# A two-layer gated cross-attention network on one core: maxima taken bank by bank and shared PSUM banks handed round differently in the second attention

## What is computed

```python
x = x + tanh(g_xattn[0]) * _L0_xattn_ref(_layernorm(x), ctx, ...)  # two attentions of 16 heads of 128, rounded to fp8
x = x + tanh(g_ffn[0])   * _L0_ffn_ref(_layernorm(x), ...)         # silu(gate) * up, 704 wide
x = x + tanh(g_xattn[1]) * _L1_xattn_ref(_layernorm(x), ctx, ctx, mask, ...)
x = x + tanh(g_ffn[1])   * _L1_ffn_ref(_layernorm(x), ...)         # 8 experts, the best one for each token

# _L1_xattn_ref: 32 heads of 8 features in 8 groups; keys and values come from ctx
q = (Q @ w_q.T).reshape(B, S, 8, 4, 8); k = (K @ w_k.T).reshape(B, S, 8, 8); v = (V @ w_v.T).reshape(B, S, 8, 8)
scores = einsum('bnghd,bmgd->bnghm', q, k) / sqrt(8)    # then the padding mask and the causal mask
out = einsum('bnghm,bmgd->bnghd', softmax(scores), v).reshape(B, S, 256)
return out @ w_o.T + b_o
```

## Time and profile before

| | us |
|---|---|
| median of 3 runs | 1426.37 (1425.85 to 1427.44) |
| the profiled execution, its own time | 1425.13 |
| its span | 1423.40 |
| PE busy in the span | 1302.0 (91%) |
| DVE, ACT, POOL busy | 1091.0, 952.1, 749.1 |
| mean granted clock of PE | 0.968 of full |

### The profile page before, as it was taken

The page is one execution under the profiler, slowest core; times in us unless marked ns, Lnnn a source line. Parts: engine busy times, 40 slices in busy tenths (PEclk is TensorE's granted clock), DMA queues, the critical chain, the costliest instruction groups (busy, mean ns, idle before and its releaser), DMA issues.

```text
span 1423.4 us, 29539 instructions
## 1 busy us (share of the span) xinstructions
PE 1302.0 (91%) x11516; PEld 1111.9 (78%) x11516; DVE 1091.0 (77%) x2141; ACT 952.1 (67%) x2110; POOL 749.1 (53%) x698
## 2 busy tenths in 40 slices
PE   1587999999999999999999999889998788996998
PEld 1577999999999999999999999767775333444998
DVE  7999888889889889889888888965345555656464
ACT  5897777877877877877887777653222454564675
POOL 5668557556557556656656643330001444453675
PEclk9699999999999999999999999999999898997899
DMA  3201010000000000000100100033544341106562
GB/s 112 60 9 30 17 23 17 16 24 16 17 23 16 24 16 16 29 11 17 31 9 16 57 2 2 16 123 51 73 73 63 69 54 46 46 2 220 181 237 96
DMA packets 59978, 69.76 MB, mean 49 GB/s; under 512 B 6811, under 2 KB 52091, under 8 KB 59712
## 3 DMA queue, kind: packets, MB, share of 16 engines
q1 hardware_dynamic: 56720, 58.64, 16.9%
q0 software_dynamic: 2944, 9.19, 1.8%
q10 hardware_dynamic: 176, 0.04, 0.0%
HBM read 55.56 MB, written 12.34 MB: 48 GB/s over the span
## 4 chain that ended last, share of the span: by engine, by line
PE 66%; DVE 16%; POOL 6%; DMA 4%; issue 4%; ACT 2%; SPq 1%; POOLq 0%; ACTq 0%; DVEq 0%
PE PC L453 7%; PE SS L419 6%; PE PO L435 5%; PE PA L387 4%; PE B L399 4%; PE PA L364 3%; PE B L1079 3%; PE PA L366 3%; PE PO L1063 2%; POOL WR L816 2%; DVE QN L700 2%; PE SS L2056 2%; PE B L2056 2%; PE B L2073 2%; PE PC L2073 2%
## 5 line engine op out<-in xcount | busy, mean ns | idle before, releaser
L873 POOL TENSOR_TENSOR RB<-YS,M 128x512 bf16<-128x512 f32 x128 | 163.5, 1277 | 254.4 <-DVE YS L726 254.4
L548 ACT ACTIVATE QT<-B,sm 128x256 f32<-128x256 f32 x256 | 131.1, 565 | 166.8 <-PE B L399 166.8
L419 PE MATMUL SS<-QT,KT 128*128 128x256 f32 x512 | 154.7, 397 | 9.4 <-DVE mx L681 9.0
L364 PE MATMUL PA<-WH,XQ 128*128 128x256 f32 x512 | 141.1, 307 | 20.9 <-POOL XQ L804 14.9
L869 POOL TENSOR_TENSOR yy<-vv,half 128x12 f32<-128x12 f32 x64 | 146.9, 2296 | 5.3
L366 PE MATMUL PA<-WL,XQ 128*128 128x256 f32 x512 | 130.3, 287 | 0.0
L1687 ACT ACTIVATE P<-PO,mcf 128x1024 f32<-128x1024 f32 x64 | 71.3, 1114 | 86.3 <-PE PO L1548 86.2
L700 DVE TENSOR_TENSOR QN<-QN,yy 128x512 f32<-128x512 f32 x128 | 122.5, 957 | 2.0 <-POOL yy L869 2.0
L1868 POOL TENSOR_SCALAR_AFFINE_SELECT P<-P 128x1024 f32<-128x1024 f32 x64 | 70.1, 1096 | 100.2 <-ACT P L1687 100.2
L681 DVE TENSOR_REDUCE mx<-SS 128x4 bf16<-128x512 f32 x128 | 88.1, 688 | 44.3 <-PE SS L411 44.2
L693 DVE TENSOR_REDUCE vv<-SQ 128x6 f32<-128x768 f32 x128 | 120.6, 943 | 0.0
(11 more groups left out here) (335 smaller groups left out, 4083.3 us busy)
## 6 DMA issues: line engine op xcount, KB each, us to landing
W<-in_w SPq DMA_DIRECT2D x16, 1024.0 KB
Q<-qsc SPq DMA_DIRECT2D x48, 128.0 KB
WR<-in_wprojT SPq DMA_DIRECT2D x16, 256.0 KB, 3.0
K<-ksc SPq DMA_DIRECT2D x12, 256.0 KB
qsc<-T POOLq DMA_DIRECT2D x8, 384.0 KB, 3.0
X<-in_x SPq DMA_DIRECT2D x4, 512.0 KB, 7.8
CR<-in_xctxT SPq DMA_DIRECT2D x8, 256.0 KB, 3.0
RSM<-rsm_d SPq DMA_DIRECT2D x16, 128.0 KB, 4.3
```

What stands on the lines that cost most here:

```text
L364: pe.matmul(PA[:, 256 * k:256 * k + 256], XQ[:, k, c, bs], wh[:, c, 256 * k:256 * k + 256], start=c == 0, stop=False)
L419: pe.matmul(SS[:, 256 * z:256 * z + 256], k[:, 128 * z:128 * z + 128], q[:, 256 * z:256 * z + 256], start=True, stop=False)
L548: a.activation(QT[i % 2][:, o:o + 256], B1[:, o:o + 256], ACT.Identity, bias=col(n + "b"), scale=col(n + "w"))
L873: p.tensor_tensor(RB[i % 2][:], YS[:], M[:], ALU.subtract).then_inc(s_rb, 1)
```

## The change

Nothing is computed otherwise; the order, the banks and the waits change.

1. `pe_shifted` in attention 0: both fp32 pairs first, then the four products with the maxima. As one bank is started only once, the second pair no longer has `start=True`.
2. `dve_maximum_1`: two reductions, one for each bank of PA, each with its own count. From step 8 on `pe_raw` waits for each half right before that half's mask product.
3. `pe_weigh_1` runs ten steps after the raw scores, not eleven, into columns 0 to 255 of B1 (even step) or B2 (odd step); `act_evac_out` copies after every step, half as much.
4. Turned maxima of blocks 2 and later go to columns 256 to 383 of B1, not to SS. The users of SS and PC move to other phases. PE's new order is, for `n % 4` = 0: raw, shifted, weigh, `pe_max_turn`, `pe_out_turn`, `pe_next_turn`; 1: raw, shifted, weigh, `pe_turn_1`, `pe_logits`; 2: raw, shifted, weigh, `pe_out_proj`; 3: raw, shifted, weigh, `pe_turn_1`. ACT copies turned maxima at the start of phase 1.
5. The queries of quarter 2 are projected behind raw step 7 into B1 and B2 (before, ahead of it into PO), those of quarter 3 turned at `n` = 9 through SS and PC (before, at 8 through B1 and B2).
6. SP loads WO and WG at `n` = 12, ahead of the queries of blocks 8 and up.
7. The routing constants are made in feed-forward 0, each in columns of its own of the scratch tile.
8. The statistics of the next layer norm are taken after each residual; the root step only gathers them, and the scaling does one block a step. SP's stores of these rows go out five steps later.

```diff
@@ pe_shifted
             for z in range(2):
                 pe.matmul(SS[:, 256 * z:256 * z + 256], k[:, 128 * z:128 * z + 128], q[:, 256 * z:256 * z + 256],
-                          start=True, stop=False)
-                for h in (2 * z, 2 * z + 1):
-                    t = pe.matmul(SS[:, 128 * h:128 * h + 128], m[:, h:h + 1].broadcast_to([128, 128]), negib[:],
-                                  start=False, stop=h % 2 == 1)
+                          start=z == 0, stop=False)
+            for h in range(4):
+                t = pe.matmul(SS[:, 128 * h:128 * h + 128], m[:, h:h + 1].broadcast_to([128, 128]), negib[:],
+                              start=False, stop=h == 3)
...
@@ turn_banks, proj_banks, dve_feed_forward_0
-            return (SS[:], PC[:]) if q4 == 2 else (B1[:], B2[:]) if q4 == 3 else PAh
+            return (SS[:], PC[:]) if q4 >= 2 else PAh
...
-            return (POa, POb) if q4 == 2 else (SS[:], PC[:]) if q4 == 3 else PAh
+            return (B1[:], B2[:]) if q4 == 2 else (SS[:], PC[:]) if q4 == 3 else PAh
...
+                    if q4 == 1 and n == 2:
+                        dve_routing_constants(v)
...
@@ sp_attention_1
-                if n == 14:
-                    sp.wait_ge(s_down, 16)
-                    sp.wait_ge(s_qst[3], 32)
+                if n == 12:
+                    sp.wait_ge(s_qp, 8)
                     sp.dma_start(WO[:], w1o.rearrange("(c p) n -> p c n", p=128)).then_inc(s_wog, 16)
                     sp.dma_start(WG[:], wgate.rearrange("(c p) n -> p c n", p=128)).then_inc(s_wog, 16)
-                if n - 2 in NEXT and n < 64:
-                    sp_next_rows(sp, NEXT[n - 2])
+                if n - 7 in NEXT and n < 64:
+                    sp_next_rows(sp, NEXT[n - 7])
@@ pe_raw
-            else:
-                pe.wait_ge(s_mx, N + i)
+            elif i < 8:
+                pe.wait_ge(s_mx, maxima_read(i - 1, 1))
...
             for half in range(2):
+                if i >= 8:
+                    pe.wait_ge(s_mx, maxima_read(i - 1, half))
                 pe.matmul(PAh[half], identb[:], MS[:, b, :].unsqueeze(1).broadcast_to([128, 4, 128]), start=True, stop=False)
@@ pe_max_turn
-            pe.matmul(SS[0:32, 256:384], mxb[b % 2][:], negib[:], start=True, stop=True).then_inc(s_mt, 1)
+            pe.matmul(maxima_bank(b)[0:32, 256:384], mxb[b % 2][:], negib[:], start=True, stop=True).then_inc(s_mt, 1)
@@ pe_weigh_1
-            if u >= 2 and e == 0:
-                pe.wait_ge(s_rt, N + u - 1)
+                if b:
+                    pe.wait_ge(s_mte, min(b + 2, NB))
+            if i < 2:
+                pe.wait_ge(s_qr, 5 + i)
+            else:
+                pe.wait_ge(s_rt, N + i - 1)
             pe.wait_ge(s_sel, i + 1)
             for x_ in range(4):
-                t = pe.matmul(OT[u % 2][32 * x_:32 * x_ + 32, 256 * e:256 * e + 256], V1[b % 2][:, g0 + x_ // 2, :],
+                t = pe.matmul(OT[i % 2][32 * x_:32 * x_ + 32, 0:256], V1[b % 2][:, g0 + x_ // 2, :],
                               of_slots(P1[i % 4])[:, x_], start=True, stop=True)
@@ act_evac_out
-            a.activation(OTS[u % 2][:], OT[u % 2][:], ACT.Copy).then_inc(s_rt, 1)
+            a.activation(OTS[u % 2][:, 256 * e:256 * e + 256], OT[e][:, 0:256], ACT.Copy).then_inc(s_rt, 1)
@@ act_attention_1, in the loop over n
+                b = every(n, 4, 5, NB)
+                if b:
+                    act_max_turned(a, b)
...
+                if 0 <= n - 11 < N1:
+                    act_evac_out(a, n - 11)
                 if 0 <= n - 8 < N1:
                     act_expo_1(a, n - 8)
@@ dve_maximum_1
-            v.tensor_reduce(mxb[b % 2][:].rearrange("p (h a) -> p h a", h=2)[:, :, 4 * d:4 * d + 4],
-                            PA[:].rearrange("p (h a m) -> p h a m", h=2, m=128), AX, ALU.max).then_inc(s_mx, 1)
+            for half in range(2):
+                o = 16 * half + 4 * d
+                v.tensor_reduce(mxb[b % 2][:, o:o + 4], PAh[half].rearrange("p (a m) -> p a m", m=128), AX,
+                                ALU.max).then_inc(s_mx, 1)
@@ dve_attention_1
-                if i == 7:
-                    dve_query_proj(v, 2)
                 dve_maximum_1(v, i)
...
+            dve_query_proj(v, 2, (0,))
...
-                if n == 40:
-                    dve_routing_constants(v)
-                u = every(n, 2, 15, 2 * NB)
+                u = every(n, 2, 14, 2 * NB)
...
                     dve_residual_1(v, b)
+                    dve_next_stats(v, b)
...
-                if n in (34, 50):
-                    dve_next_scale(v, NEXT[n - 2], next_bs[NEXT[n - 2]])
+                for k in range(2):
+                    if 16 * k + 34 <= n < 16 * k + 38:
+                        dve_next_scale(v, k, (n - 12 * k - 34,))
```

More of the change, by code:

```diff
@@ L1388, in build @@
         WO = sb("WO", [128, 2, H])
+        fill0 = sb("fill0", [128, 4096])
         V1 = [sb(f"V1{i}", [128, G, 32]) for i in range(2)]
-        fill2 = sb("fill2", [128, 1024])
+        OTS = [sb(f"OTS{i}", [128, 512]) for i in range(2)]
         AO = [sb(f"AO{i}", [128, H]) for i in range(2)]
@@ L1431, in next_count, with maxima_read, maxima_bank @@
         def next_count(b):
-            return 8 + (b // 4 + 1 if b < 8 else b - 5 if b < 12 else 7 + (b == 15))
+            return 8 + (b + 1 if b < 12 else 13 + (b == 15))
+        def maxima_read(i, half):
+            return N + 2 * i + half + 1
+        def maxima_bank(b):
+            return SS if b < 2 else OT[0]
         def next_bank(b):
@@ L1518, in pe_raw @@
                 o = 128 * (2 * g2 + pp)
-                t = pe.matmul(PAh[half][:, o:o + 128], Q6[r, of_block(b)[0], 2 * (g0 + g2) + pp, of_block(b)[1]], K6[r, g0 + g2, tok_],
-                              start=False, stop=m >= 6)
+                t = pe.matmul(PAh[half][:, o:o + 128], Q6[r, of_block(b)[0], 2 * (g0 + g2) + pp, of_block(b)[1]],
+                              K6[r, g0 + g2, tok_], start=False, stop=m >= 6)
             t.then_inc(s_S, 1)
         def pe_max_turn(pe, b):
-            pe.wait_ge(s_mx, N + 4 * b + 4)
+            pe.wait_ge(s_mx, maxima_read(4 * b + 3, 1))
             if b:
@@ L1634, in pe_attention_1 @@
                     pe_shifted_1(pe, n - 8)
-                b = every(n, 4, 5, NB)
+                if 0 <= n - 10 < N1:
+                    pe_weigh_1(pe, n - 10)
+                b = every(n, 4, 4, NB)
                 if b is not None:
                     pe_max_turn(pe, b)
-                if n == 8:
+                if n == 9:
                     pe_query_turn(pe, 3)
@@ L1641, in pe_attention_1 @@
                     pe_query_proj(pe, 3)
-                if 0 <= n - 11 < N1:
-                    pe_weigh_1(pe, n - 11)
+                b = every(n, 4, 16, NB)
+                if b is not None:
+                    pe_out_turn(pe, b)
+                b = every(n, 4, 36, 8)
+                if b is not None:
+                    pe_next_turn(pe, b)
+                u = every(n, 2, 13, 2 * NB)
+                if u is not None:
+                    pe_turn_1(pe, u)
                 b = every(n, 4, 37, 8)
@@ L1648, in pe_attention_1 @@
                     pe_logits(pe, n - 64)
-                b = every(n, 4, 17, NB)
-                if b is not None:
-                    pe_out_turn(pe, b)
                 b = every(n, 4, 18, NB)
@@ L1654, in pe_attention_1 @@
                     pe_out_proj(pe, b)
-                b = every(n, 4, 35, 8)
-                if b is not None:
-                    pe_next_turn(pe, b)
                 if 70 <= n < 74:
                     pe_next_turn(pe, n - 62)
-                u = every(n, 2, 14, 2 * NB)
-                if u is not None:
-                    pe_turn_1(pe, u)
             pe_logits(pe, 11)
@@ L1843, in dve_attention_1 @@
             dve_residual_1(v, 15)
+            dve_next_stats(v, 15)
             dve_next_root(v, 4)
```

134 lines of the change are left out of this document (61 added, 73 removed).

## The result

The changed kernel takes 1391.88 us (median of 4 executions, 1388.72 to 1395.58), the kernel before 1426.11 us (median of 4, 1424.99 to 1427.44). The ratio is 0.9761, with a 95% interval of 0.9730 to 0.9791: 34 us faster, where 29 were forecast (1397 us, range 1387 to 1410). The profiled execution of the changed kernel took 1388.72 us with a span of 1387.0 us, 3 us under its median; the spans differ by 36.4 us.

A forecast was written before the change was run, and what follows sets the result against it. PE was taken as the bound, busy 1302.0 of 1423.4 us, so gains must cut its work or gaps. 6 + 0 + 6.5 + 15 + 1.5 = 29 us gave 1397 us, range 1387 to 1410.

The forecast's parts named there:

- Attention 0: Adjacent fp32 pairs avoid a weight load behind short bf16 products, 0.06 us a step: 6 us, between 0 and 7.7.
- The loop of DVE: Attention 1: with split maxima DVE's loop is 2.12 us, under every phase of PE, so not the bound.
- the split's gain is the 14.9 us of waits, in part: Attention 1: two reductions in place of one would remove part of PE's 14.9 us of waits.
- The rival in which DVE pays 64 x 0.15 = 10 us: Attention 1: DVE becomes the bound and splits are paid in full, 1407 us; chance 0.22 together with the uneven clock.
- Start of attention 1: PE's 3.51 us wait at step 8 goes, 3.3 us of idle before shifted product 1 comes: net 0, between -3 and +3.
- the fourth rival: Low-clock periods of 3.4 us persist, each costing about 1.5; four give 1403 us; chance 0.22 together with DVE as bound.
- they, not PE, decide when step 32 goes on: Query transfers of attention 1 bind up to step 32, which goes on at 1167.5: gain 6.5 us.
- The queue's hole: SP's DMA queue empty from 1142 to 1146; closing this 4.5 us was forecast; if it stayed, the gain would be 3.
- Steps 33 to 63: Later attention 1: 78.5 against 93.6 us, a gain of 15, between 9 and 17.
- a block costs PE its own work, 10.73 - 0.32 - 0.18: Quiet four-step block of attention 1: PE's work is conserved, 10.23 us, taken as 10.2.
- the allowance for a scaling in a short step and a period of low clock: Steps 33 to 63: 2.3 us left for a scaling (0.64) meeting a short step and one low-clock period.
- Slower: Attention 1: weigh products, now two steps behind their exponential, wait for POOL's chain; at 0.5 us a step 1429; chance 0.05.

The follow-up runs named there:

- both repairs: Changed kernel with DVE's query chains cut in two and query transfers sent in parts of three DMAs: ratio 0.9681, 1380.59 us.
- the second profiled execution: The changed kernel run once more, nothing altered, as the measure for runs on the same chip: ratio 0.9792, median 1396.57 us.
- cut chains: Changed kernel with DVE's part of the query chains cut into two calls with a maximum between them: ratio 0.9704.
- one maximum: Changed kernel with one maximum over both banks in place of two (edit 2 undone alone): ratio 0.9783.
- extras apart: Changed kernel with the next layer's turns and logits ahead of the weigh product, not behind other fp32 products: ratio 0.9807.
- the constants at step 40: Changed kernel with the routing constants made at step 40 again (edit 7 undone alone): ratio 0.9817.
- thinning the transfers alone: Changed kernel with query transfers in parts of three DMAs behind blocks 2 to 9, not whole halves behind blocks 2 to 5: ratio 0.9752.

## Why the prediction was right

**Attention 0**: right in mechanism and size. 6.5 us in this trace, 5.3 in that of the kernel with this edit alone and 6.7 by its median, against 6. The first fp32 product of the second pair held PE for 0.27 us before the change and holds it for 0.22 now, which fits an fp32 weight load (0.19 us, where a bf16 load takes 0.10) that no longer stands behind a short product.

**The loop of DVE**: right that it isn't the bound; the pair of maxima takes 1.29 us as computed, and DVE waits for PE before three pairs of four. But what the split brings was overstated: "the split's gain is the 14.9 us of waits, in part" becomes 1.2 us in steps 33 to 63. These waits went, as far as the runs tell, with the long and short phases that edits 3 and 4 evened out. The rival in which DVE pays 64 x 0.15 = 10 us also had too high a price: a pair keeps DVE for 1.29 us and one maximum for 1.23, so it is 64 x 0.06 = 4 us at most.

**Start of attention 1**: right for the new wait (3.3 forecast, 3.46 measured) and for its net of about zero on the spot. What failed is the silence on what follows: the 6.8 us at half clock behind this wait, and after the wait at step 13, which the kernel before had too, another 20.5, where it had 6.8. Only the fourth rival, "the clock stays as uneven as now", spoke of it, and with four periods of 3.4 us.

**The transfers**: the step "they, not PE, decide when step 32 goes on" was wrong for the changed kernel. The queue's hole was not the limit and no shifted product waited for maxima; PE was slower than the transfers because of the clock. The size came out (6.4 against 6.5) by luck, by two errors that cancel: without the half clock PE would have reached step 33 sooner (the start takes 103.9 us with both repairs instead of 112.7), and with it the transfers had time. In the second profiled execution the same stretch gains 9.4 us. The kernels with cut chains and with one maximum show the forecast waits, so the mechanism exists one layer below the one that decided. That WO and WG cost 2.5 us was true of the kernel before and is not true of this one in either order.

**Steps 33 to 63**: 73.7 against 78.5, the largest miss, and outside the range given for this term (gain 9 to 17, measured 19.9). Of the 4.8 us, 2.5 are the block: 9.83 us, not 10.2, in 27 / 4 blocks. The step that failed is "a block costs PE its own work, 10.73 - 0.32 - 0.18": it took each product's share of PE as fixed wherever it stands. The kernel with extras apart gives 10.16 us a block, the forecast's 10.2; the position behind other fp32 products is worth 0.33. The rest, 2.3 us, is the allowance for a scaling in a short step and a period of low clock, which didn't come: the stretch 1165 to 1235 has a clock of 1.00 throughout.

**The constants**: the 3.43 us of wait and the slow stretch behind them were rightly taken as one thing; 9.5 and 8.7 us in the traces, 5.7 and 3.6 us by the medians. Nothing was paid in feed-forward 0.

**Tail**: 1.6 against 1.5. **Slower**, by weigh products that wait for POOL: no such wait in the list of the changed kernel.

In the sum the traces gave 7.4 us more than forecast: 4.9 in steps 33 to 63, 0.5 in attention 0, 2.4 before it and in feed-forward 0, -0.4 elsewhere. The median lies 3.2 us above the profiled execution, where it lay 1.0 above it before, which takes 2 us back; so 34 us stand against 29.

## What to carry to other kernels

Price a wait with the stretch behind it: here waits of PE of 3.4, 3.0 and 1.5 us had 10.2, 13.7 and 20.5 us at half clock at or behind their end, and a cut in a chain of another engine that took 2.5 us of waits away made the kernel 8 to 12 us faster by its medians. Price a product by its neighbours too: the four small fp32 products of the logits hold PE a third less (0.36 against 0.54 us) behind other fp32 products than behind bf16 ones. And where two limits lie close (clock and transfers here), remove them together before judging either, since thinning the transfers alone brought nothing that could be told from the spread. And look at a second profiled execution before explaining a stretch: the start took 112.7 and 109.6 us in two of the same kernel.

## What the runs showed of the hardware

**DVE's small casts can stand behind POOL.** In the kernel with the constants at step 40, DVE, then POOL:

```profile
1183.64 0.23 DVE L1794 CAST tri<-ti 128x128 bf16<-128x128 f32 x1 [2.19 <-POOL ti L1892]
1183.78 1.06 DVE L1797 CAST order<-ti 128x8 f32<-128x8 int32 x1
...
1184.89 0.65 DVE L1797 CAST spare<-ti 128x16 f32<-128x16 int32 x1
...
1183.69 1.12 POOL L1879 TENSOR_SCALAR_AFFINE_SELECT P<-P 128x1024 f32<-128x1024 f32 x1
1184.79 0.72 POOL L1874 TENSOR_TENSOR X<-X,BO 128x256 f32<-128x256 f32 x1
```

A cast of eight columns takes 1.06 us and ends with POOL's clearing of 1.12 us; in feed-forward 0, where POOL is idle, the same cast takes 0.16 us. The cast of 16 columns at 1184.89 likewise takes 0.65 us and ends with POOL's next instruction, against 0.17. Together with the 2.19 us for POOL's lists that is most of what DVE loses there.

The Trainium skill, "SBUF — State Buffer", section "Terms", calls the port pair of VectorE and GpSimd exclusive, held for the full instruction, so that the loser "fully blocks"; this pair of rows agrees with it (1.06 us beside 0.16).

**Two maxima cost nearly what one does.** One maximum of 1024 columns took 1.21 to 1.23 us, two of 512 columns in a row 1.27 to 1.29 us together, though each alone takes 0.69.

The Trainium skill, "VectorE: DVE Perf Modes", section "Side-by-side: where the cycles go for N=2048 bf16", gives some 150 cycles of fixed cost per instruction at 0.96 GHz. By an estimate from that figure the pair would occupy DVE for 0.16 us more; for two that don't depend on each other the trace shows 0.06.

**Half clock after short waits.** PE fell to 1.2 GHz near the end of a wait of 3.01 us (constants at step 40) and, at 1107 us of the changed kernel, 0.8 us behind one of 1.50, and stayed there for 13.7 and 20.5 us while it was busy almost without a gap (15.00 of 15.00 us in 1110 to 1125). How long this lasts differs between executions with the same waits: 20.5 and 13.7 us in the two of the changed kernel, 13.7 to 23.9 in the variants that are the same up to there, with starts of 109.4 to 120.5 us (the longest also holds a wait for MT). The executions of the changed kernel spread over 14 us on one chip, those with the chains cut over 13, those with cut chains and thinned transfers over 5; how much of that is the clock isn't shown.
